# Output products of three value heads made from two rounded parts, one core

## The reference

```python
Q = x @ Wq ; K = ctx @ Wk ; V = ctx @ Wv            # 8 heads of 512
score = einsum('bhqd,bhkd->bhqk', Q, K) / sqrt(512)
attn  = softmax(where(mask, score, -inf))
out   = einsum('bhqk,bhkd->bqhd', attn, V).reshape(B, -1, 4096) @ Wo + x
out   = (out - mean) * rsqrt(var + 1e-5) * gamma + beta
```

## Time and profile before

| | |
|---|---|
| median of three runs | 355.64 us |
| the profiled execution | 355.74 us, span 353.9 us |
| PE busy | 347.4 us (98%) |
| DVE, ACT, POOL busy | 269.7, 230.3, 192.9 us |
| key heads | up to about 65 us of the span |
| value heads (8 to 15) | about 65 to 124.5 us |
| stage over x | from about 124.5 us |

### The profile page before, as it was taken

How to read it: one execution, slowest core, us unless ns; L and a number is a source line. 1 busy time by engine, 2 the same in 40 slices (tenths; PEclk the granted TensorE clock), 3 DMA queues, 4 the chain that set the end, 5 groups by cost and what they waited for, 6 DMA issues and landing times. The chain is left out here.

```text
span 353.9 us, 6790 instructions
## 1 busy us (share of the span) xinstructions
PE 347.4 (98%) x2271; PEld 323.8 (91%) x2271; DVE 269.7 (76%) x501; ACT 230.3 (65%) x780; POOL 192.9 (55%) x208
## 2 busy tenths in 40 slices
PE   8999999999999999999999999999999999999994
PEld 6999999999999999898899899989988998999884
DVE  3299998673921267898798988987987989889896
ACT  3377764154333569887876976878768769768560
POOL 0045650000003856689679688688696796885243
PEclk9999999999999999999999999999999999999999
DMA  8998669776635070052242341541432423413012
GB/s 251 416 422 315 267 225 343 266 260 216 219 129 219 0 265 34 1 181 92 89 150 70 138 150 41 171 142 38 180 97 84 149 70 139 149 42 109 31 50 100
DMA packets 19682, 55.80 MB, mean 158 GB/s; under 512 B 1728, under 2 KB 3264, under 8 KB 17728
## 3 DMA queue, kind: packets, MB, share of 16 engines
q1 hardware_dynamic: 18784, 54.38, 42.8%
q10 hardware_dynamic: 864, 1.00, 1.0%
HBM read 46.98 MB, written 8.39 MB: 156 GB/s over the span
## 5 line engine op out<-in xcount | busy, mean ns | idle before, releaser
L644 PE MATMUL pair<-vw_hi,pt_hi 128*128 128x512 f32 x155 | 62.2, 401 | 0.0
L644 PE MATMUL pair<-vw_hi,pt_lo 128*128 128x512 f32 x155 | 60.9, 393 | 0.0
L644 PE MATMUL pair<-vw_lo,pt_hi 128*128 128x512 f32 x155 | 60.6, 391 | 0.0
L1249 POOL TENSOR_TENSOR out_sb<-centred,beta_sb 128x512 f32<-128x512 f32 x30 | 38.8, 1294 | 29.0 <-ACT centred L839 28.9
L1269 POOL TENSOR_TENSOR x_sum<-xt_in 128x256 f32<-128x256 f32 x16 | 11.9, 744 | 63.9 <-DMA xt_in<-x_tiles 63.7
L794 ACT ACTIVATE prob<-c,neg_max 128x77 f32<-128x77 f32 x128 | 43.9, 346 | 0.0
L1294 POOL TENSOR_TENSOR xo_lo<-x_sum,xo_hi 128x512 fp32r<-128x512 f32 x32 | 41.4, 1299 | 0.5 <-ACT xo_hi L818 0.5
L569 PE MATMUL pair<-a_hi,xo_hi 128*128 128x308 f32 x128 | 40.4, 316 | 0.0
L569 PE MATMUL pair<-a_hi,xo_lo 128*128 128x308 f32 x128 | 38.9, 304 | 0.0
L569 PE MATMUL pair<-a_lo,xo_hi 128*128 128x308 f32 x128 | 38.9, 304 | 0.0
L832 ACT ACTIVATE pt_hi<-pair 128x640 fp32r<-128x640 f32 x32 | 22.5, 703 | 23.3 <-PE pair L631 23.3
(11 more groups left out here) (117 smaller groups left out, 955.7 us busy)
## 6 DMA issues: line engine op xcount, KB each, us to landing
w_out<-wo SPq DMA_DIRECT2D x8, 1024.0 KB, 4.8
xt_in<-x_tiles SPq DMA_DIRECT2D x16, 512.0 KB, 4.1
x_in<-x_rows SPq DMA_DIRECT2D x16, 512.0 KB, 4.8
out<-out_sb SPq DMA_DIRECT2D x31, 256.0 KB, 2.2
w_out<-wq_t SPq DMA_DIRECT2D x7, 1024.0 KB, 6.9
w_proj<-wv SPq DMA_DIRECT2D x8, 768.0 KB, 4.6
w_proj<-wk SPq DMA_DIRECT2D x6, 768.0 KB, 9.3
w_out<-wq_t SPq DMA_DIRECT2D x2, 512.0 KB, 7.6
```

What stands on the lines that cost most here:

```text
L644: mm = pe.matmul(ps_out[:, i % 2, 0:s.model], ps[:, j, :], v[:, b, j, :], start=(j == 0 and n == 0), stop=(j == s.key_t - 1 and n == len(p ...
L1249: pool.tensor_tensor(out_sb[i % OUT_RING][:, :], centred[i % 2][:, :], beta_sb[:, :], ALU.add)\
```

## The change

Output products of uses 12, 13 and 14 (value heads 4, 5 and 6) take the short form. The whole value buffers are placed so that `v_t[n]` lies over the start of `kv_t[n]`, since a short use and a whole use now alternate in them. The copies of the result become two steps: ACT copies `first(pair)` to `vw_t`, then DVE adds `second(pair)` in `add_out_product`, and those who waited for ACT's copy wait for DVE's addition.

```diff
+    SPLIT_VALUES = range(H + 4, USES - 1)
...
-            v_t = [values.enter_context(nc.sbuf_tensor(f"v_t{n}", [P, s.dim_t, s.toks], F32)) for n in range(2)]
+            v_t0 = values.enter_context(nc.sbuf_tensor("v_t0", [P, s.dim_t, s.toks], F32))
+            values.enter_context(nc.sbuf_tensor("gap6", [P, s.dim_t, s.toks], F32))
+            v_t = [v_t0, values.enter_context(nc.sbuf_tensor("v_t1", [P, s.dim_t, s.toks], F32))]
...
         def whole_out(u):
-            return u < FULL_OUT or u >= H
+            return u < FULL_OUT or (u >= H and u not in SPLIT_VALUES)
+        def split_before(u):
+            return sum(not whole_out(v) for v in range(u))
+        def summed_before(u):
+            return 2 * sum(not whole_out(v) for v in range(H, u))
...
             def wait_out(u, half):                                  # PE
                 if u < H:
                     pe.wait_ge(dve_a_lo, 2 * u + half + 1)
-                else:
-                    pe.wait_ge(act_vw_t, 2 * (u - H) + half + 1)
+                elif whole_out(u):
+                    pe.wait_ge(act_vw_t, 2 * (u - H) + half + 1)
+                else:
+                    pe.wait_ge(dve_vw_sum, summed_before(u) + half + 1)
...
             def out_product(u):                                     # PE
...
+                    if m == 2 and u >= H:
+                        transpose_vw(u - H)
...
             def transpose_vw(h):
                 for j, b in plan[h]:
                     pe.wait_ge(act_vw_t, 2 * h)
+                    pe.wait_ge(dve_vw_sum, summed_before(H + h))
...
                 if u >= H:                                          # ACT
                     split_vw(u - H)
-                if u + 1 < H:
+                if u + 1 < USES and not whole_out(u + 1):
                     round_w_out(u + 1)
                 take_out_product(u, 1)
...
+            def add_out_product(u, half):                           # DVE
+                cols = head_cols(vw_t, half, u - H)
+                dve.wait_ge(act_vw_t, 2 * (u - H) + half + 1)
+                dve.tensor_tensor(cols, by_batch(second(ps_outp[half])), cols, ALU.add).then_inc(dve_vw_sum, 1)
...
             for u in range(USES):                                   # DVE
-                if u + 1 < H:
+                if u + 1 < USES and not whole_out(u + 1):
                     split_kv(u + 1)
                 if u < H:
...
                 else:
+                    if not whole_out(u):
+                        add_out_product(u, 0)
                     if u == USES - 1:
                         bias_rows()
                     split_vw(u - H)
+                    if u + 1 < USES and not whole_out(u + 1):
+                        split_w_out(u + 1)
+                    if not whole_out(u):
+                        add_out_product(u, 1)
                 if u == H:
...                                                                 # right_sum, split_t as before
```

More of the change, by code:

```diff
@@ L247, in build @@
         dve_comb, dve_half_max = sem("dve_comb"), sem("dve_half_max")
+        dve_vw_sum = sem("dve_vw_sum")
         dve_centred, dve_zero, dve_pad, dve_last = sem("dve_centred"), sem("dve_zero"), sem("dve_pad"), sem("dve_last")
@@ L476, in wait_kv @@
                 else:
-                    pe.wait_ge(dve_kv_lo, 2 * (u - FULL_OUT) + half + 1)
+                    pe.wait_ge(dve_kv_lo, 2 * split_before(u) + half + 1)
             def project_full(u):
@@ L539, in out_product @@
                     if m % 2 == 0:
-                        pe.wait_ge(act_o_hi, 2 * (u - FULL_OUT) + half + 1)
-                        pe.wait_ge(dve_o_lo, 2 * (u - FULL_OUT) + half + 1)
+                        pe.wait_ge(act_o_hi, 2 * split_before(u) + half + 1)
+                        pe.wait_ge(dve_o_lo, 2 * split_before(u) + half + 1)
                         wait_out(u - 1, half)
@@ L936, in split_w_out @@
                 for half in range(2):
-                    dve.wait_ge(act_o_hi, 2 * (u - FULL_OUT) + half + 1)
+                    dve.wait_ge(act_o_hi, 2 * split_before(u) + half + 1)
                     dve.tensor_tensor(half_cols(w_out_lo[u % W_RING], half), half_cols(w_out_sb[u % W_RING], half),
@@ L1154, in _ @@
                     take_out_product(u, 0)
-                    if u + 1 < H:
+                    if not whole_out(u + 1):
                         split_w_out(u + 1)
```

## The result

The changed kernel takes 357.09 us (median of 6 runs, 356.81 to 357.29) against 355.84 us (6 runs, 355.55 to 356.09) for the kernel before: ratio 1.0028, 95% interval 1.0018 to 1.0039, 1.25 us slower. 357.1 was forecast, as 1.4 us more than a median of 355.64 us from three runs; the six runs give 355.84. So the loss was forecast 0.15 us too large and the base stood 0.20 us too low, and that the two make the measured time to the tenth is luck. In the table of the experiments two of e6's twelve executions, disturbed ones of 431.51 and 579.83 us at mean granted clocks of 0.755 and 0.56, are left out.

A forecast was written before the change was run, and what follows sets the result against it. PE, 98% busy, was taken to bound the kernel. Use 12 adds 1.61 us (late start 0.31, wait 1.45, saving -0.11 and -0.04), uses 13 and 14 -0.20: together +1.4, 357.1 us; range 356.2 to 358.0.

The forecast's parts named there:

- Step 1: DVE's split of the values of use 12, in use 11: projection 13 starts 0.31 us late.
- The hand-over from DVE to PE: Time from the end of a DVE split to PE's first weight load behind it: 0.24 us.
- Step 2: Rounding and splitting the weights of use 12: first half done at 98.59 us, PE does not wait.
- Steps 3 and 4: T4 and T3 splits end at 102.58 us, then use 13's value split; use 12's transposes wait 1.45 us.
- Step 5: Uses 13 and 14: no wait of PE, smallest cover 1.2 us.
- The saving: Short output products on PE in the value heads: 0.15 us saved a head, 0.45 us for three.
- The 0.1 us for cuts by the transposes: Transposes cutting the product in uses 12 and 13: 0.1 us lost for both together, between -0.1 and +0.2.
- A: Rival: short product's saving follows column count, 0.8 us a head, 355.5 us, not slower; chance 0.04.
- B: Rival: the transposes of use 12 are not late, 355.6 us; chance 0.07.
- C: Rival: second wait in use 14, DVE's weight split stretched beside POOL's sums, about 0.9 us more, 358.0 us; chance 0.08.
- D: Rival: PE's clock falls to 1.2 GHz over one output product, another 4 us, 361 us; chance 0.01.

The follow-up runs named there:

- e6: Changed kernel with use 13's value split moved ahead of the T3 splits and use 12's between the two T3 sums; 355.78 us, ratio 0.9995.
- e1: Changed kernel, but DVE splits the values of use 13 before the T4 and T3 splits instead of behind them; 356.16 us, ratio 1.0004.
- e10: The same kernel as e6, run again for a usable profile; 355.73 us, ratio 0.9998.
- e2: Changed kernel with only use 12 in the short form, uses 13 and 14 full; 356.06 us, ratio 1.0005.
- e9: e4 with twelve matmuls of zeros on PE ahead of the transposes of use 12; 359.00 us, ratio 1.0082.
- e7: Changed kernel with one more 128x512 addition on DVE ahead of the T splits; 358.90 us, ratio 1.0094.
- e5: Changed kernel, but PE uses full matmuls on the high parts in uses 12 to 14, ACT and DVE unchanged; 357.35 us, ratio 1.0044.
- e8: Changed kernel with two more 128x512 additions on DVE ahead of the T splits; 359.80 us, ratio 1.0098.
- e4: Changed kernel with three more 128x512 additions on DVE ahead of the T splits; 360.73 us, ratio 1.0135.

## Why the prediction was right

The forecast (one wait of PE in use 12 for the values of use 13) came out, by its own steps:

- *Step 1.* The split of the values of use 12 held up projection 13: it starts 95.94 - 91.53 = 4.41 us behind use 11's product, before 4.20: 0.21 late where 0.31 was said. The hand-over from DVE to PE was too large in the sum. It was read at the first short use, 0.24 us; here it is 95.94 - (95.32 + 0.47) = 0.15 us and 103.57 - (102.57 + 0.86) = 0.14 us. Why it was longer at the first short use, where PE waits for several results, was not tried.
- *Step 2.* Weights done at 97.45 + 1.22 = 98.67 (98.59 said), no wait seen. The product began 3.12 us behind projection 13, not 3.04: the second matmul of the delayed projection came 0.21 us behind its first instead of 0.13 (its row is 3.38 us long, not 3.31). e1's projection, late in the same way, has the same 0.21, and e10's, which is not late, has 0.13 and takes 3.04 us. So the late start cost 0.21 + 0.08 = 0.29 us in all, which is also the difference between the stretches of e1 and e10 (0.30). In the changed kernel itself it only shortens the wait that follows, since DVE's chain sets the start of the transposes; where that wait is gone, in e1 and e2, it is what is left of the loss.
- *Steps 3 and 4.* T splits until 102.65 (102.58), values until 103.43 (103.35), transposes at 103.57 (103.59). PE's arrival is 99.06 plus the 3.15 us that the same three tiles take in use 13 (111.67 - 108.52): 102.21 (102.14). The wait is 1.36 us (1.45). e1 shows that the order made it, e9 and e7 that DVE's chain counts one to one, e2 that the wait needs the short use 13.
- *Step 5.* No wait in uses 13 and 14. They take 113.55 - 105.48 = 8.07 and 120.73 - 113.55 = 7.18 us. Before, use 13 took 8.22, and a full pair without transposes takes 7.35: 0.15 and 0.17 are saved. Projection 14 started at 105.48, inside the bounds that the prediction set for itself (104.5 and 106.5).
- *The saving.* 0.15 us a head, shown by e5. The 0.1 us for cuts by the transposes was a term that is not there: in use 13 transposes and last tile take 113.55 - 111.67 = 1.88 us, in use 12 before 1.93. It and the hand-over, both some 0.1 us too large, are why the stretch grew by 1.20 and not 1.4.
- *Rivals.* A is refuted by e5, B by the wait itself. Under A the Trainium skill was quoted too simply: in "TensorE: Matmul & The Clock Gate" (section Back-to-back issue gap) N/2.4 + 2.5 ns is the distance of a matmul by itself, and the section says that at small N it falls short for a stream of weight loads and matmuls. The trace agrees with that: in use 14 the 16 steps of the short form take 120.73 - 116.60 = 4.13 us, 258 ns each, not 197. Of C the cause was there: the weights of use 14 took 2.91 us for two (2.36 in use 12), beside POOL, but they were done at 117.28, and PE, which began the product at about 116.6, needs their second half only 2 us after that; it did not wait. D did not happen, but in e8 1.2 us more of wait were enough for it in four of six executions; a chance of 0.01 was too small. Its price was too large: the fallen clock cost 1.6 us, not 4.

## What to carry to other kernels

Before work is added to an engine with room on average, look at each place where its order puts the new instructions behind old ones, and ask which wait of the bound engine stands behind the last of them; here 2.93 us of T splits, harmless before, made a wait of 1.36 us, three times what the change could save (0.45). The cure was the order of two instructions; it took the loss away, and what it won beyond that (0.20 us of the stretch in e1, 0.50 with both splits moved in e10) is too small for the times to show. And when two forms of a product are compared, take the distance of starts over whole groups in the same mixture, since columns alone promised 0.8 us a head and the real saving was 0.15.

## What the runs showed of the hardware that was not expected

PE's granted clock fell to 1.2 GHz behind a wait of 2.42 us (e8) and of 3.03 us (e4), each time 0.4 to 0.6 us after PE had gone on working, and stayed there for about 3.5 us, which cost 1.6 us; behind 1.22 us (changed kernel) and 1.83 us (the profiled execution of e7) it stayed at 2.4 GHz. In e8 two of six executions were as fast as if it had stayed, which suggests that the length of the wait alone does not decide; only one of the six has a profile, and nothing further was tried. Where the clock falls, the wait costs more than its own length, and filling it with matmuls of zeros gave 1.7 us back (e9, on the same chip as e4; e7 and e8 ran on another).
